# Four build steps' high one-hots in one VectorE operation, read by TensorE at every fourth element

## The chip, the core and the metric

The kernel runs on one core of a Trainium2 chip. The metric is the device time of one execution in microseconds; the lowest is the best. The core's engines are TensorE (PE, with PEld for loading its weights), VectorE (DVE), ScalarE (ACT), GpSimd (POOL) and SyncE (SP), each with its own instruction stream in order, which wait for one another by semaphores.

## The reference, cut to what matters

A graph of 6250 nodes has 200,000 edges, sorted by target. Three graph-convolution layers run over layer-normed node features of width 256, then a feed-forward layer over the half of the nodes that a router chooses.

```
def _gcn_conv(x, W, b, src, dst, norm, num_nodes):
    h = x @ W
    msg = h[src] * norm[:, None]
    agg = jax.ops.segment_sum(msg, dst, num_segments=num_nodes)
    return agg + b
...
h = jax.nn.relu(_gcn_conv(x, W1, b1, src, dst, norm, num_nodes))
h = jax.nn.relu(_gcn_conv(h, W2, b2, src, dst, norm, num_nodes))
return _gcn_conv(h, W3, b3, src, dst, norm, num_nodes)
...
x = x + _L0_gnn_ref(_layernorm(x, axis=-1), ...)
x = x + _L0_ffn_ref(_layernorm(x, axis=-1)[None], ...)[0]
```

## The kernel before

**The graph as a matrix.** The nodes lie in 49 tiles of 128. For the first 34 target tiles, which hold most edges, the kernel builds the adjacency matrix as counts (source in tile on the partitions, one row of 49 x 128 numbers a target tile) and multiplies it with the node features; the other tiles gather their edges' rows with indirect DMAs. The edges come in steps of 128. A target tile is cut into windows of 4 or 3 targets, and each window has a fixed quota of steps. In a build step (`step`, L1250) TensorE multiplies two one-hots of the step's 128 edges: the low one-hot `olo` (128 columns, source within its tile) as weights, the high one-hot `ohi` (49 source tiles x 4 or 3 targets, 196 or 147 columns) as moving operand, and adds into a PSUM window. ScalarE takes finished groups of windows out of PSUM (L1627, `evac_group`).

**Who writes the one-hots.** VectorE, in `one_hots(j)`, one call for each pair j of steps. Every even pair writes `olo` for four steps (L891): an is_equal of a table `iota_many`, in which each of 128 numbers stands four times, with four columns of `slo`, broadcast. Every pair writes `ohi` for its two steps (L894) in the same manner, from `iota_two`, in which each number stands twice. The results of a call are interleaved: the elements of one step stand four (`olo`) or two (`ohi`) apart. TensorE reads its operands at that distance. The ring holds RING = 8 pairs; the semaphore `used` counts steps that TensorE has done and `hot` the pairs that VectorE has written.

**The order of the work.** There are 1011 pairs. The first (the scan, j below SCAN) are built among the preparation of edges, degrees and first-layer products; VectorE's list there holds `unpack`, `digits`, `low_first` (L906) and others between the one-hots. From then on TensorE's list is written out by hand: after each pair come the units (dense matmuls of 512 columns, L1283, or gathered ones, L1295) that the table `DUE` names. VectorE's list follows the same table: after the one-hots of pair j come `sum_tile` (L923, L925), `low_tile` (L930) and `spot_steps` (L941) that are due by pair j - 5. The first sum of a layer frees the PSUM bank of the next unit.

**The overflow round.** At one place of each layer (`spill`) the kernel adds edges that did not fit a quota. GpSimd fetches an item and its rows (indirect DMAs L1849 to L1864; L1864 gathers rows of `row_dram`, which SyncE has stored before), compares (L1866 to L1870), and TensorE multiplies (L1326) at a fixed place of its list; all three engines of the round wait for one another. After it GpSimd goes on to `fetch_row` (L1890), the gathers of the sparse tiles.

**Other lines that are spoken of.** L1184 is the reciprocal of the roots of the degrees, for which ScalarE's L1731 must be done; L902 adds self-loops.

Of the kernel before, what the change touches and what calls it, by code (L numbers as in the profile page):

```python
# [8 lines left out]
ALU = mybir.AluOpType  # L9
# [3 lines left out]
F16 = mybir.dt.float16  # L13
# [3 lines left out]
P = 128  # L17
# [3 lines left out]
TILES = -(-N // P)  # L21
# [14 lines left out]
WC = W * TILES  # L36
# [14 lines left out]
WIDTH = [min(WIDTH_OF[t], P - i) for t in range(TD) for i in range(0, P, WIDTH_OF[t])]  # L51
# [17 lines left out]
WINDOW_OF = {FIRST[w] + i: w for w in range(WN) for i in range(QUOTA[w])}  # L69
# [49 lines left out]
RING = 8  # L119
# [4 lines left out]
HOTS = 24  # L124
# [302 lines left out]
def graph(nc, ctx, space, gathered_in, ones, route, small, smalli, b1_sb, br_b, x, x_turned, dst_rows, dst_over, dst_last, edges, gw, gb, wr, br, w1, b1, w2, b2, pair_dram, out):  # L427
    def sb(name, shape, dt=F32):
        return ctx.enter_context(nc.sbuf_tensor(name, shape, dt))
# [7 lines left out]
    area_a, area_b, area_r, area_t, area_g, area_w = (space[n][:] for n in ("a", "b", "ring", "tables", "rows", "work"))  # L437
# [9 lines left out]
    at = ET + 1 + ETILES  # L447
# [6 lines left out]
    at = (W + 1) * SBASE // 2  # L454
# [11 lines left out]
    at = 11 * D  # L466
# [23 lines left out]
    hots_area = sb("hots", [P, HOTS // 4, P, 4], F16)  # L490
    hots_f = hots_area[:].rearrange("p s n i -> p (s n i)").bitcast(F32)
    bias_rows = [hots_f[:, 0:D], area_w[:, 5 * D:6 * D]]
    key = area_t[:, 0:SBASE // 2].bitcast(F16)
    slo = area_t[:, SBASE:SBASE + SBASE // 2].bitcast(F16)
    at = SBASE + SBASE // 2
    ohi = area_t[:, at:at + RING * WC].bitcast(F16).rearrange("p (r n i) -> p r n i", r=RING, i=2)
    olo = area_t[:, at + RING * WC:at + RING * (WC + P)].bitcast(F16).rearrange("p (r n i) -> p r n i", r=RING // 2, i=4)
    at = TILES * P // 2
    xn = area_t[:, at:at + KC * D].rearrange("p (i d) -> p i d", i=KC)
# [26 lines left out]
    key_s, src_s = sb("key_s", [P, CHS * P], F16), sb("src_s", [P, CHS * P], I32)  # L526
    gw_sb, gb_sb = sb("gw_sb", [P, 3, HALVES, D]), sb("gb_sb", [P, 3, HALVES])
    ident, ident16, ones16 = sb("ident", [P, P]), sb("ident16", [P, P], F16), sb("ones16", [P, P], F16)
    zeros16 = sb("zeros16", [P, P], F16)
    iota16, iota_many = sb("iota16", [P, WC], F16), sb("iota_many", [P, P, 4], F16)  # L530
    iota_two = sb("iota_two", [P, WC, 2], F16)
    per_node = sb("per_node", [P, 8, TILES])
    dinv, factor, unfactor = per_node[:, 0], per_node[:, 1:4], per_node[:, 4:7]
    moments = sb("moments", [P, D])
# [28 lines left out]
    at = 0  # L563
# [4 lines left out]
    at = TILES * P  # L568
# [3 lines left out]
    at = len(BLOCKS[0]) * 2 * D  # L572
# [74 lines left out]
    pw = [ps(f"pw{i}", [P, 2, 512]) for i in range(2)]  # L647
# [42 lines left out]
    with nc.Block() as block:  # L690
        @block.vector
        def _(dve):
            def noted(ins, name=None):
                steps["all"] += 1
                if name:
                    steps[name] = steps["all"]
                ins.then_inc(c_dve, 1)

            def done(ins, name=None):
                noted(ins, name)  # L700
                dve.wait_ge(c_dve, steps["all"])
# [66 lines left out]
            lows(slice(0, 1))  # L768
            dve.wait_ge(c_pool, CONSTANTS + LATER_CONSTANTS)
            place_steps(0)  # L770
            done(dve.tensor_copy(iota_many[:], iota16[:, 0:P].unsqueeze(2).broadcast_to([P, P, 4])))
            noted(dve.tensor_copy(iota_two[:], iota16[:].unsqueeze(2).broadcast_to([P, WC, 2])))
            picks(False)

            def scales(l, bound):
# [106 lines left out]
                                            apply_absolute_value=True))  # L882

            def one_hots(j):
                r = j % RING
                if j >= RING:
                    dve.wait_ge(used, 2 * (j - RING + (2 if j % 2 == 0 else 1)))
                for t in LOOPS_OF.get(j, ()):
                    add_loops(t)
                if j % 2 == 0:  # L890
                    dve.tensor_tensor(olo[:, r // 2], iota_many[:], slo[:, 2 * j:2 * j + 4].unsqueeze(1).broadcast_to([P, P, 4]),  # L891
                                      ALU.is_equal)
                n = TILES * max(WIDTH[WINDOW_OF.get(2 * j + i, 0)] for i in range(2))
                dve.tensor_tensor(ohi[:, r, 0:n], iota_two[:, 0:n], key[:, 2 * j:2 * j + 2].unsqueeze(1).broadcast_to([P, n, 2]),  # L894
                                  ALU.is_equal).then_inc(hot, 1)

            def add_loops(n):
                dve.wait_ge(evac, PER_TILE * (n + 1))
# [34 lines left out]
            def spot_steps(n):  # L933
                if n == 0:
                    dve.wait_ge(stored_0, 16)
                    dve.wait_ge(stored_s, 32)
                    dve.wait_ge(pairs_clear, 16 * len(LATE_RUNS))
                if n >= HOTS // 4:
                    dve.wait_ge(g_used, SPOT_GROUPS[n - HOTS // 4][1])
                s = STEP_TILE[SPOT_GROUPS[n][0]]  # L940
                dve.tensor_tensor(hots_area[:, n % (HOTS // 4)], iota_many[:], key_s[:, s:s + 4].unsqueeze(1).broadcast_to([P, P, 4]),  # L941
                                  ALU.is_equal).then_inc(spot, 1)

            def measure():
# [275 lines left out]
        def _(pe):  # L1220
# [19 lines left out]
            def step(s):  # L1240
                w, j, i = WINDOW_OF[s], s // 2, s % 2
                v = GROUP_OF[w]
                t, a, b = EGROUPS[v]
                if s == FIRST[a] and v >= 2:
                    pe.wait_ge(evac, v - 1)
                if i == 0:
                    pe.wait_ge(hot, j + 1)
                half, at_c = (w - a) // PER_BANK[WIDTH_OF[t]], (w - a) % PER_BANK[WIDTH_OF[t]] * WIDTH_OF[t] * TILES
                n = WIDTH[w] * TILES
                pe.matmul(pw[v % 2][:, half, at_c:at_c + n], olo[:, j % RING // 2, :, j % 2 * 2 + i], ohi[:, j % RING, 0:n, i],  # L1250
                          start=s == FIRST[w], stop=s == FIRST[w] + QUOTA[w] - 1, skip_group_check=True).then_inc(used, 1)

            def pair(j):
# [854 lines left out]
```

## Time and profile before

| | |
|---|---|
| time of the runs, median of 3 (lowest, highest) | 1947.01 us (1945.54, 1950.79) |
| span of the profiled execution | 1945.7 us |
| PE busy | 1843.1 us (95%), 10171 matmuls |
| DVE busy | 1059.8 us (54%), 3304 instructions |
| ACT busy | 530.8 us (27%) |
| POOL busy | 1188.0 us (61%) |
| mean granted TensorE clock | 0.968 |
| build steps, L1250 | 2022 |
| high one-hots, L894 | 1011, 300.5 us busy, mean 330 ns |
| low one-hots, L891 | 506, 212.8 us busy, mean 420 ns |

The profiled execution's own time is its span and the little that lies around it: the median of the runs is 1.3 us above the span. Busy times are those of the whole span; which engine is late differs from stretch to stretch. A duration in the profile reaches from an instruction's start to its end, and the next one on the engine may start before that end, so what an instruction costs its engine in a full list is the distance between starts.

### The profile page before, as it was taken

To read this page: it belongs to the slowest core of one execution; us is meant where nothing else is said; L and a number is where in the kernel's file an instruction comes from. 1 tells how busy PE (TensorE), PEld (TensorE's weight loads), DVE (VectorE), ACT (ScalarE), POOL (GpSimd) and SP (SyncE) were. 2 spreads that over 40 slices of the span, in tenths; PEclk is the share of its full clock that TensorE was granted. 3 is DMA by queue.
4 is the path that set the end of the run, shared out by engine and by line. 5 is a ranking of instruction groups with operands and counts; after the bars stand their busy time and mean duration, and the time that the engine had idled before them with its cause. 6 is when DMAs were issued, how large, how long until landed. Compare 5 with 4: busy or idle time off the path is not lost.

```text
span 1945.7 us, 28922 instructions
## 1 busy us (share of the span) xinstructions
PE 1843.1 (95%) x10171; PEld 1070.5 (55%) x10171; DVE 1059.8 (54%) x3304; ACT 530.8 (27%) x1127; POOL 1188.0 (61%) x1178
## 2 busy tenths in 40 slices
PE   6875889999999999999999999999999999989998
PEld 5753556666555666645555555554444444446755
DVE  7777989888666666542222222213554456876422
ACT  5734234444444455512111111110000000002021
POOL 5401787688777676437777777745777777731301
PEclk9965889999999999999999999999999999999999
DMA  7568235555655566577677667756878888752200
GB/s 267 161 224 279 83 124 181 183 166 171 213 198 194 201 209 214 184 254 247 229 241 255 231 233 235 256 178 234 314 268 316 302 313 296 265 159 94 81 14 23
DMA packets 170453, 403.42 MB, mean 207 GB/s; under 512 B 29419, under 2 KB 122529, under 8 KB 157640
## 3 DMA queue, kind: packets, MB, share of 16 engines
q1 hardware_dynamic: 119720, 263.44, 37.9%
q0 software_dynamic: 50592, 138.13, 22.8%
q8 instruction: 85, 1.39, 0.3%
q14 instruction: 56, 0.46, 0.1%
HBM read 282.57 MB, written 118.89 MB: 206 GB/s over the span
## 4 chain that ended last, share of the span: by engine, by line
PE 84%; DVE 6%; issue 3%; POOL 3%; ACT 2%; DMA 1%; POOLq 0%; DVEq 0%; another core or an unknown queue 0%; ACTq 0%
PE ag L1283 29%; PE pw L1283 21%; PE ag L1295 10%; PE pw L1250 6%; PE pw L1379 3%; POOL space_rows L1864 2%; PE pw L1311 2%; PE both L1311 2%; PE ag L1392 2%; PE pw L1392 2%; PE ag L1379 2%; PE both L1303 1%; DVE space_tables L894 1%; PE ag L1236 1%; ACT space_ring L1627 1%
## 5 line engine op out<-in xcount | busy, mean ns | idle before, releaser
L1890 POOL DMA_INDIRECT space_rows<-row_dram,src_s x947 | 1006.4, 1063 | 335.3 <-issue 208.9
L1283 PE MATMUL ag<-space_a,space_ring 128*128 128x512 f16 x2107 | 623.2, 380 | 1.2 <-DVE space_work L925 1.1
L1250 PE MATMUL pw<-space_tables 128*128 128x147 f16 (+1 forms) x2022 | 330.0, 248 | 47.8 <-DVE space_tables L894 40.9
L1295 PE MATMUL ag<-space_rows,hots 128*128 128x512 f16 x947 | 358.5, 379 | 0.0
L1250 PEld LDWEIGHTS pw<-space_tables 128*128 128x128 f16 x2022 | 218.9, 116 | 233.1 <-DVE space_tables L894 65.1
L894 DVE TENSOR_TENSOR space_tables<-iota_two,space_tables 128x294 f16<-128x294 f16 (+1 forms) x1011 | 300.5, 330 | 0.0
L1627 ACT ACTIVATE space_ring<-pw 128x784 f16<-128x784 f32 (+1 forms) x257 | 220.4, 858 | 291.0 <-PE pw L1250 285.7
L1283 PEld LDWEIGHTS ag<-space_a,space_ring 128*128 128x128 f16 x2107 | 198.2, 97 | 99.8 <-DVE space_work L925 1.3
L891 DVE TENSOR_TENSOR space_tables<-iota_many,space_tables 128x512 f16<-128x512 f16 x506 | 212.8, 420 | 25.3 <-PE pw L1250 23.0
L1283 PE MATMUL pw<-space_b,space_ring 128*128 128x512 f16 x735 | 190.9, 379 | 0.0
L1283 PE MATMUL pw<-space_a,space_ring 128*128 128x512 f16 x686 | 168.7, 379 | 0.0
L1637 ACT ACTIVATE space_work<-space_work,per_node 128x256 f32<-128x256 f32 x147 | 73.8, 503 | 320.7 <-DMA space_work<-extra 320.6
L1295 PEld LDWEIGHTS ag<-space_rows,hots 128*128 128x128 f16 x947 | 107.3, 113 | 78.7
L930 DVE SCALAR_TENSOR_TENSOR space_a<-pw,per_node,space_a 128x256 f16<-128x256 f32 x49 | 23.7, 484 | 219.4 <-ACT space_a L1651 208.0
L1645 ACT ACTIVATE space_work<-both,gb_sb 128x128 f32<-128x128 f32 x196 | 61.3, 365 | 228.6 <-PE both L1303 228.4
L1283 PE MATMUL ag<-space_b,space_ring 128*128 128x512 f16 x441 | 115.9, 379 | 0.0
L1283 PEld LDWEIGHTS pw<-space_b,space_ring 128*128 128x128 f16 x735 | 71.8, 98 | 78.2
L1283 PEld LDWEIGHTS pw<-space_a,space_ring 128*128 128x128 f16 x686 | 67.3, 98 | 78.0
L941 DVE TENSOR_TENSOR hots<-iota_many,key_s 128x512 f16<-128x512 f16 x238 | 106.2, 459 | 1.3
L923 DVE SCALAR_TENSOR_TENSOR space_work<-ag,per_node,space_work 128x256 f32<-128x256 f32 x78 | 37.5, 481 | 101.6 <-PE ag L1283 57.5
L930 DVE SCALAR_TENSOR_TENSOR space_b<-both,per_node,space_b 128x256 f16<-128x256 f32 x49 | 23.7, 484 | 110.2 <-ACT space_b L1651 110.2
L1283 PE MATMUL pw<-space_a,space_tables 128*128 128x512 f16 x294 | 77.8, 388 | 0.0
(421 smaller groups left out, 1973.0 us busy)
## 6 DMA issues: line engine op xcount, KB each, us to landing
space_ring<-adj SPq DMA_DIRECT2D x48, 1568.0 KB, 7.5
adj<-space_ring SPq DMA_DIRECT2D x34, 1568.0 KB, 6.1
space_tables<-adj SPq DMA_DIRECT2D x17, 1568.0 KB, 7.8
extra<-hots SPq DMA_DIRECT2D x3, 6272.0 KB, 22.4
space_work<-extra SPq DMA_DIRECT2D x147, 128.0 KB
space_rows<-row_dram,src_s POOLq DMA_INDIRECT x947, 3.4
space_b<-in_x_turned SPq DMA_DIRECT2D x7, 896.0 KB, 13.6
space_a<-in_x SPq DMA_DIRECT2D x7, 896.0 KB, 6.1
```

What stands on the lines that cost most here:

```text
L891: dve.tensor_tensor(olo[:, r // 2], iota_many[:], slo[:, 2 * j:2 * j + 4].unsqueeze(1).broadcast_to([P, P, 4]), ALU.is_equal)
L894: dve.tensor_tensor(ohi[:, r, 0:n], iota_two[:, 0:n], key[:, 2 * j:2 * j + 2].unsqueeze(1).broadcast_to([P, n, 2]), ALU.is_equal).then_inc ...
L941: dve.tensor_tensor(hots_area[:, n % (HOTS // 4)], iota_many[:], key_s[:, s:s + 4].unsqueeze(1).broadcast_to([P, P, 4]), ALU.is_equal).the ...
L1250: pe.matmul(pw[v % 2][:, half, at_c:at_c + n], olo[:, j % RING // 2, :, j % 2 * 2 + i], ohi[:, j % RING, 0:n, i], start=s == FIRST[w], sto ...
L1283: mm = pe.matmul(bank(q), a[:, k, :], hh[l][:, k, :], start=i == 0 and not own, stop=i == TILES - 1)
L1295: pe.matmul(bank(q), hots_area[:, hot_at, :, g - SPOT_GROUPS[SPOT_GROUP_OF[g]][0]], slots[g % GR], start=False, stop=i == n).then_inc(g_us ...
L1311: mm = pe.matmul(ph[l - 1], fresh[:, q % 2, f, :], gw_sb[:, l, f, :], start=f == 0, stop=f == HALVES - 1)
L1379: mm = pe.matmul(bank_of(hidden_banks[h % 3])[:, 0:n], w1_sb[:, k, m * P:(m + 1) * P], xt[c][:, k, 0:n], start=k == 0, stop=k == HALVES - 1)
L1392: mm = pe.matmul(bank_of(out_banks[s % 2])[0:n, 0:D], hid[c % 2][:, m, i * P:i * P + n], w2_sb[:, m, :], start=m == 0, stop=m == HM - 1)
L1627: act.activation(target[:, :, d:d + n].rearrange("p s (h d) -> p s h d", h=2), pw[v % 2][:, :, 0:n // 2 * TILES].rearrange("p h (d s) -> p ...
L1637: act.activation(ep[:, q % 2], ep[:, q % 2], ACT.Copy, scale=unfactor[:, l, t:t + 1]).then_inc(e_scaled, 1)
L1890: pool.indirect_dma_start(slots[g % GR], None, row_dram[STEP_LAYER[g]], bass.IndirectOffsetOnAxis(src_s[:, s:s + 1], 0)).then_inc(g_in[g % ...
```

## The change

The high one-hots of four steps, two pairs, are written by one operation in place of two. The table `iota_two` goes; a table `iota_four` of 196 numbers, each four times, takes its place, and `iota_many` becomes its first 128 numbers. The ring keeps its size: 4 slots of four steps in place of 8 of two. Odd calls of `one_hots` write nothing and wait for nothing (they still add self-loops where those are due). The operation is as wide as the widest window of its four steps. `hot` counts groups of four steps, and TensorE waits for it once in four steps. TensorE reads the moving operand at every fourth element where it read every second. Weights, step order, windows and everything else stay.

```
-    ohi = area_t[:, at:at + RING * WC].bitcast(F16).rearrange("p (r n i) -> p r n i", r=RING, i=2)
+    ohi = area_t[:, at:at + RING * WC].bitcast(F16).rearrange("p (r n i) -> p r n i", r=RING // 2, i=4)
...
-    iota16, iota_many = sb("iota16", [P, WC], F16), sb("iota_many", [P, P, 4], F16)
-    iota_two = sb("iota_two", [P, WC, 2], F16)
+    iota16, iota_four = sb("iota16", [P, WC], F16), sb("iota_four", [P, WC, 4], F16)
+    iota_many = iota_four[:, 0:P]
...
-            done(dve.tensor_copy(iota_many[:], iota16[:, 0:P].unsqueeze(2).broadcast_to([P, P, 4])))
-            noted(dve.tensor_copy(iota_two[:], iota16[:].unsqueeze(2).broadcast_to([P, WC, 2])))
+            done(dve.tensor_copy(iota_four[:], iota16[:].unsqueeze(2).broadcast_to([P, WC, 4])))
...
             def one_hots(j):
-                r = j % RING
-                if j >= RING:
-                    dve.wait_ge(used, 2 * (j - RING + (2 if j % 2 == 0 else 1)))
+                r = j % RING // 2
+                if j % 2 == 0 and j >= RING:
+                    dve.wait_ge(used, 2 * (j - RING + 2))
                 for t in LOOPS_OF.get(j, ()):
                     add_loops(t)
                 if j % 2 == 0:
-                    dve.tensor_tensor(olo[:, r // 2], iota_many[:], slo[:, 2 * j:2 * j + 4].unsqueeze(1).broadcast_to([P, P, 4]),
+                    dve.tensor_tensor(olo[:, r], iota_many, slo[:, 2 * j:2 * j + 4].unsqueeze(1).broadcast_to([P, P, 4]),
                                       ALU.is_equal)
-                n = TILES * max(WIDTH[WINDOW_OF.get(2 * j + i, 0)] for i in range(2))
-                dve.tensor_tensor(ohi[:, r, 0:n], iota_two[:, 0:n], key[:, 2 * j:2 * j + 2].unsqueeze(1).broadcast_to([P, n, 2]),
-                                  ALU.is_equal).then_inc(hot, 1)
+                    n = TILES * max(WIDTH[WINDOW_OF.get(2 * j + i, 0)] for i in range(4))
+                    dve.tensor_tensor(ohi[:, r, 0:n], iota_four[:, 0:n], key[:, 2 * j:2 * j + 4].unsqueeze(1).broadcast_to([P, n, 4]),
+                                      ALU.is_equal).then_inc(hot, 1)
...
-                if i == 0:
-                    pe.wait_ge(hot, j + 1)
+                if s % 4 == 0:
+                    pe.wait_ge(hot, s // 4 + 1)
...
-                pe.matmul(pw[v % 2][:, half, at_c:at_c + n], olo[:, j % RING // 2, :, j % 2 * 2 + i], ohi[:, j % RING, 0:n, i],
+                pe.matmul(pw[v % 2][:, half, at_c:at_c + n], olo[:, j % RING // 2, :, j % 2 * 2 + i], ohi[:, j % RING // 2, 0:n, j % 2 * 2 + i],
```

## Rows read from the trace of the kernel before

**Rows 1.** Busy us (instructions) by stretch: PE, PEld, DVE, ACT, POOL; clock, DMA.

```profile
200.20:249.00 48.80, 46.69 (x327) 28.12 (x326) 48.80 (x181) 12.51 (x16) 43.98 (x1) 0.89 0.14 53
...
256.00:262.00 6.00, 6.00 (x25) 3.48 (x25) 2.72 (x6) 2.09 (x3) 2.56 (x3) 0.51 0.06 20
262.00:281.50 19.50, 17.74 (x145) 12.02 (x143) 19.31 (x75) 6.96 (x10) 17.27 (x3) 1.00 0.54 210
281.50:823.00 541.50, 537.26 (x3413) 340.69 (x3414) 397.71 (x1305) 261.34 (x423) 385.15 (x329) 1.00 0.57 191
```

**Rows 2.** Waits from 205 to 249 us: waited for, total us, times, longest.

```profile
PEld pw L1250 <- DVE space_tables L894: 10.5, 38, 0.4
```

**Rows 3.** Timeline of VectorE, 157 to 165 us: start, duration, idle time before.

```profile
164.22 0.47 DVE L1184 RECIPROCAL per_node<-per_node 128x49 f32<-128x49 f32 x1 [6.58 <-ACT per_node L1731]
```

**Rows 4.** Timeline of TensorE around the overflow round and at the first sum.

```profile
248.92 0.38 PE L1283 MATMUL ag<-space_a,space_ring 128*128 128x512 f16 x1
255.84 0.58 PE L1326 MATMUL both<-space_rows 128*128 128x512 f16 x1 [6.54 <-POOLq L1827]
...
281.54 0.39 PE L1283 MATMUL ag<-space_a,space_ring 128*128 128x512 f16 x1 [1.11 <-DVE space_work L925]
```

**Rows 5.** GpSimd: timeline of 205 to 300 us, and the page's group of L1890.

```profile
205.02 47.81 POOL L1864 DMA_INDIRECT space_rows<-row_dram,space_rows  x1 [36.41 <-DMA row_dram<-space_a]
...
264.77 16.70 POOL L1890 DMA_INDIRECT space_rows<-row_dram,src_s  x1 [0.99 <-POOL space_rows L1883]
...
L1890 POOL DMA_INDIRECT space_rows<-row_dram,src_s x947 | 1006.4, 1063 | 335.3 <-issue 208.9
```

**Rows 6.** Timeline of VectorE where the one-hots pause, 251 to 282 us.

```profile
251.43 0.59 DVE L894 TENSOR_TENSOR space_tables<-iota_two,space_tables 128x392 f16<-128x392 f16 x2
257.62 0.91 DVE L891 TENSOR_TENSOR space_tables<-iota_many,space_tables 128x512 f16<-128x512 f16 x1 [5.61 <-PE pw L1250]
...
281.00 0.48 DVE L925 SCALAR_TENSOR_TENSOR space_work<-ag,per_node,space_work 128x256 f32<-128x256 f32 x1
```

**Rows 7.** Timeline of VectorE in two stretches of nothing but one-hots.

```profile
216.74 0.42 DVE L891 TENSOR_TENSOR space_tables<-iota_many,space_tables 128x512 f16<-128x512 f16 x1
217.08 0.53 DVE L894 TENSOR_TENSOR space_tables<-iota_two,space_tables 128x294 f16<-128x294 f16 x2
217.52 0.42 DVE L891 TENSOR_TENSOR space_tables<-iota_many,space_tables 128x512 f16<-128x512 f16 x1
...
239.63 0.42 DVE L891 TENSOR_TENSOR space_tables<-iota_many,space_tables 128x512 f16<-128x512 f16 x1
239.97 0.64 DVE L894 TENSOR_TENSOR space_tables<-iota_two,space_tables 128x392 f16<-128x392 f16 x2
240.51 0.42 DVE L891 TENSOR_TENSOR space_tables<-iota_many,space_tables 128x512 f16<-128x512 f16 x1
```

**Rows 8.** Busy time by stretch of L891 alone, one per four steps.

```profile
166.30:200.20 33.90, 5.89 (x14) 0.50 1.00 330
200.20:249.00 48.80, 25.41 (x60) 0.89 0.14 53
```

**Rows 9.** Timeline of TensorE, 240.5 to 241.8 us.

```profile
240.59 0.38 PE L1283 MATMUL ag<-space_a,space_ring 128*128 128x512 f16 x1
240.81 0.34 PE L1250 MATMUL pw<-space_tables 128*128 128x196 f16 x2
240.99 0.38 PE L1283 MATMUL ag<-space_a,space_ring 128*128 128x512 f16 x1
```

**Rows 10.** Groups of weight loads, 281.5 to 823 us: busy us, mean ns, idle before.

```profile
L1250 PEld LDWEIGHTS pw<-space_tables 128*128 128x128 f16 x1414 | 159.5, 114 | 145.3 <-ACT space_ring L1627 9.3 <-DVE space_tables L894 0.8
L1283 PEld LDWEIGHTS ag<-space_a,space_ring 128*128 128x128 f16 x1381 | 126.7, 96 | 34.0 <-DVE space_work L925 1.3 <-issue 0.3
```

**Rows 11.** Groups of matmuls of the build in the same stretch.

```profile
L1250 PE MATMUL pw<-space_tables 128*128 128x196 f16 x864 | 146.8, 250 | 1.9 <-ACT space_ring L1627 1.9
L1250 PE MATMUL pw<-space_tables 128*128 128x147 f16 x537 | 81.3, 230 | 2.2 <-ACT space_ring L1627 2.1
```

More of the change, by code:

```diff
@@ L940, in spot_steps @@
                 s = STEP_TILE[SPOT_GROUPS[n][0]]
-                dve.tensor_tensor(hots_area[:, n % (HOTS // 4)], iota_many[:], key_s[:, s:s + 4].unsqueeze(1).broadcast_to([P, P, 4]),
+                dve.tensor_tensor(hots_area[:, n % (HOTS // 4)], iota_many, key_s[:, s:s + 4].unsqueeze(1).broadcast_to([P, P, 4]),
                                   ALU.is_equal).then_inc(spot, 1)
```

## The prediction

> **What bounds the kernel now.** I read the table of busy time by stretch first. The graph is built by 2022 "build steps" on TensorE, each multiplying a low one-hot (weights) with a high one-hot (moving operand); VectorE writes the one-hots, so the question in each stretch is which of the two is late. From 200.2 to 249 us VectorE is busy for 48.80 of 48.8 us while TensorE has idle left; from 281.5 us to the end of the build at 823 us TensorE is busy for 537.26 of 541.5 us and VectorE has 144 us free [rows 1]. So a cheaper VectorE can pay only before 281.5 us, and a dearer TensorE read is paid after it. The waits of 205 to 249 us say the same: TensorE's weight loads wait 38 times for the high one-hots of L894, 10.5 us in all [rows 2].
>
> Before 164 us the kernel is a chain of many engines. VectorE then stands idle for 6.58 us until ScalarE's root at L1731, which hangs on a round trip through GpSimd and DMA [rows 3]. Whatever VectorE gains earlier is spent in that wait, so I count nothing before 164 us.
>
> The odd place is 249 to 256 us. TensorE's last matmul starts at 248.92 us and the next only at 255.84 us, after 6.54 us of waiting for GpSimd's queue (the overflow round, "spill") [rows 4]. GpSimd's list shows why it is late: its gather at L1864 takes 47.81 us, while the same kind of instruction at L1890 takes 1.06 us on average over 947 of them [rows 5]. It starts at 205.02 us and ends at 252.83 us, 0.8 us after VectorE's uninterrupted one-hots end (251.43 + 0.59 = 252.02 us) [rows 5, 6]. The next long one ends at 264.77 + 16.70 = 281.47 us, just as VectorE's L925, which reads PSUM, ends at 281.48 us [rows 5, 6]. So in this trace a gather gets through when VectorE pauses from operations that read two SBUF tensors. The stall then sits where it does because TensorE stops, the ring of one-hots fills, VectorE halts and GpSimd is let in: it moves with TensorE's arrival.
>
> **The change, part by part.** *One high one-hot operation for two.* In the stretch with 147-column steps a group of four steps (one L891, two L894) takes VectorE 217.52 - 216.74 = 0.78 us; with 196 columns it takes 240.51 - 239.63 = 0.88 us [rows 7]. The two differ by 2 x 98 elements, so an element costs 0.10/196 = 0.00051 us. L891, whose operands have exactly the new operation's form (fourfold table, fourfold broadcast, 512 elements), takes 0.34 us start to start [rows 7], of which elements are 0.26; 0.07 to 0.08 us is fixed. The new operation keeps the elements and drops one fixed part: 0.07 us less for each group of four steps, 0.71 and 0.81 us in place of 0.78 and 0.88. That L891 runs at the same price per element excludes that the wider form falls to a slower rate.
>
> How many groups count: 14 between 166.3 and 200.2 us, 60 up to 249 us [rows 8], and 3 more while the ring's other slots fill. In the first stretch VectorE also has two other operations per pair and now and then waits for ScalarE, but those waits hang on VectorE's own earlier writes and move with it. 77 x 0.07 = 5.4 us earlier at 256 us. This holds only while TensorE can follow: two steps of 196 columns take 240.99 - 240.81 = 0.18 us and the dense matmul between pairs 240.81 - 240.59 = 0.22 us [rows 9], so four steps with two of those need 0.79 to 0.80 us against VectorE's new 0.81. It can, with almost nothing to spare.
>
> From 262 to 281.5 us VectorE is busy for 19.31 of 19.5 us [rows 1], and it ends with the tile's sum, for which TensorE waits 1.11 us [rows 4]. VectorE would be 23 x 0.07 = 1.6 us earlier, and TensorE gets the 1.1 us that it waited, no more. After that nothing: what VectorE saves from there on falls into its own free time.
>
> *The wait for the ring.* An odd pair waited for the same number of steps as the even pair before it (2(j - 6) in both), so dropping its wait frees nothing. Four slots of four steps hold what eight of two held. *Coarser hand-over.* The first pair of a group now gets its one-hot one half operation later (0.15 to 0.20 us, its extra elements), the second no later. Where TensorE waits for VectorE anyway the group's end decides, and it is earlier; where TensorE is the bound, VectorE is ahead in the ring and this costs nothing. *The table.* One copy of 784 elements replaces 512 and 392 before 164 us: nothing. Quads that straddle windows of unequal width write some columns more; there are few.
>
> *The moving read, every fourth element.* No row shows a moving operand read so. Below 0 there is no reason for it. The lower bound is 0: the present read of every second element makes 0.18 us for two steps of 196 columns, 0.09 each, and a contiguous 512-column matmul at 0.22 us scales to 0.084 [rows 9]; the doubling from one to two thus cost at most 0.006 us, part of it for loading weights. The upper bound is from weights that are already read at every fourth element: 114 ns a load against 96 contiguous, for 128 columns [rows 10], 0.14 ns a column, or 20 ns for 147 and 27 ns for 196 columns. For the 864 and 537 steps after 281.5 us [rows 11] that is 23.3 + 10.7 = 34 us. I take 0, because the moving read itself is the nearest row. One nanosecond a step would be 1.4 us; about 4.6 ns eat the whole gain.
>
> Row and rule differ here. The weights read at every fourth element are 18 ns dearer than contiguous ones [rows 10]. The Trainium skill ("Advanced Engine Details and Errata", SBUF Cachelines) asks for two hits on each 16-byte line for full speed and warns of a penalty where every access meets another line; f16 values at every fourth place leave exactly two. By the rule the sum below stays; by the row it ends 34 us higher. No run here shows the moving read itself.
>
> *Sum.* The profiled execution's span is 1945.7 us; the runs' median of 1947.0 lies 1.3 above. 5.4 + 1.1 = 6.5 us less gives 1939.2 for the span and **1940.5 us** for the median, 0.33% less. The measurement tells 0.3%, 5.8 us, from no change, so even the forecast lies near that edge.
>
> **Rivals.** *A: the strided read costs (the other side).* Place: TensorE's 1414 steps after 281.5 us, where nothing covers it. For: weights at that stride are dearer [rows 10]. Against: they are the only such sign. At 10 ns a step: 14.1 - 6.5, about 1955 us; at the upper bound 1974. It decides from 4.6 ns on, and is told from no change from 8.7 ns.
>
> *B: the overflow round does not move.* If L1864's 47.81 us is the gather's own time and not VectorE's doing, GpSimd still lets TensorE go at 255.8 us, less only the microsecond by which the gather may start earlier. Then the 5.4 us turn into a longer wait and 1.1 to 2.1 us remain: about 1945 us. For: GpSimd was waiting for a store's landing just before. Against: the two ends that meet VectorE's pauses [rows 5, 6].
> The Trainium skill ("SBUF — State Buffer", Who interferes with whom) speaks for B: it infers that a tensor_tensor takes only the shared read port and so does not hold up the writing of descriptors. In the trace the gather fares otherwise, 47.81 against 1.06 us, and the measurement decides for me.
>
> *C: GpSimd is let in early.* With 0.81 against 0.79 us a group VectorE is almost no longer the bound; if it fills the ring once between 205 and 249 us, the gather ends then and TensorE's gap of 6.7 us (255.84 - 248.92 less one matmul) goes too, and with it part of the 6 us at half clock that follow (granted 0.51) [rows 1, 4]. VectorE's own 5.61 us of idle time there [rows 6] is what can be used: 6 to 9 us more, 1932 to 1934 us. Against: at 0.02 us a group the ring does not fill in 60 groups.
>
> **How the numbers follow.** Forecast 0.57 (1938 to 1943), A 0.16, B 0.17, C 0.10. The bound for faster is 1941.2 us: the forecast gives 0.35 faster and 0.22 same, C 0.10 faster, B 0.17 same, A 0.13 slower and 0.03 same. So faster 0.45, same 0.42, slower 0.13. The range takes in C's lower end and B and cuts off most of A: 1931 to 1949.
>
> **What would show it.** Right: the high one-hots number 506 at about 0.46 and 0.56 us each (durations overlap the next start by about 0.08), groups at 0.71 and 0.81 us; TensorE's stall at the overflow round still some 7 us long but starting near 243.5 us; the sum's wait at 281.5 us gone; the build steps of 196 columns still 0.09 us apart. Wrong: build steps further apart between 300 and 823 us (A); the spill matmul still at 255 us after a longer wait (B); L1864 far shorter than 40 us and no gap (C).

## The result and the profile after

| | before | after |
|---|---|---|
| median of the runs (lowest, highest) | 1947.54 us (1945.54, 1950.79), 4 runs | 2064.02 us (2063.67, 2064.92), 4 runs |
| span of the profiled execution | 1945.7 us | 2062.4 us |
| build steps on TensorE: busy, mean | 330.0 us, 248 ns | 465.1 us, 324 ns |
| last build step starts at | 822.8 us | 938.9 us |

The changed kernel is slower by a factor of 1.0595 (95% interval 1.0578 to 1.0611): 116.5 us, where 6.5 us less were forecast. The last row of the table tells where to look: 116 of the 117 us of span are there when the build ends.

The busy time by stretch, as in [rows 1] (PE, PEld, DVE, ACT, POOL; clock, DMA):

```profile
200.20:249.00 48.80, 47.67 (x282) 32.43 (x283) 43.39 (x110) 10.87 (x14) 7.54 (x6) 0.92 0.15 58
...
281.50:823.00 541.50, 538.18 (x2858) 334.95 (x2857) 325.40 (x818) 209.47 (x343) 278.83 (x267) 1.00 0.46 155
```

From 281.5 us on TensorE is as full as before and at the same granted clock of 1.00, but in the same 541.5 us it gets through 2858 matmuls in place of 3413. So it waits no more than before; pieces of its work take longer. And before 249 us, where VectorE was the late engine, VectorE now has 5.4 us free and TensorE is the late one. The timeline of TensorE shows which piece; beside it [rows 9] has the same place before the change:

```profile
239.77 0.40 PE L1282 MATMUL ag<-space_a,space_ring 128*128 128x512 f16 x1
240.01 0.52 PE L1249 MATMUL pw<-space_tables 128*128 128x196 f16 x2
240.34 0.40 PE L1282 MATMUL ag<-space_a,space_ring 128*128 128x512 f16 x1
240.58 0.51 PE L1249 MATMUL pw<-space_tables 128*128 128x196 f16 x2
```

Two steps of 196 columns take 240.34 - 240.01 = 0.33 us (0.18 in [rows 9]), and the dense matmul behind them 0.24 (0.22). Worked out from the starts of all matmuls between 300 and 1000 us, a step of 196 columns costs 0.158 us before another step and 0.175 before a dense matmul (0.090 and 0.087 before the change), one of 147 columns 0.116 and 0.134 (0.069 and 0.067), and the dense matmul behind a pair 0.236 (0.215). Its own operands haven't changed, but the profile shows its weight loads longer too, 111 ns on average where [rows 10] has 96, while those of the build steps are as they were. Why the matmul behind a pair is longer was not tested. The weight loads (busy us, mean ns, idle before):

```profile
L1249 PEld LDWEIGHTS pw<-space_tables 128*128 128x128 f16 x1429 | 162.1, 114 | 151.8 <-ACT space_ring L1626 9.3
L1282 PEld LDWEIGHTS ag<-space_a,space_ring 128*128 128x128 f16 x1389 | 154.2, 111 | 70.1 <-DVE space_work L924 0.3
```

The sum comes near the loss. After 281.5 us there are 864 steps of 196 columns at 78 ns more (67 us), 551 of 147 at 57 ns (31 us), and behind some 707 pairs a dense matmul at 21 ns (15 us): 113 us. Step 600 starts 5.28 us later than before and the last one 116.15, so 110.9 us were lost in between.

GpSimd's gather of the overflow round is short now and TensorE no longer stops for it ([rows 4, 5]: 47.81 us, and 6.54 us of waiting):

```profile
204.63 5.36 POOL L1863 DMA_INDIRECT space_rows<-row_dram,space_rows  x1 [34.53 <-DMA row_dram<-space_a]
```

```profile
256.87 0.40 PE L1282 MATMUL ag<-space_a,space_ring 128*128 128x512 f16 x1
257.11 0.38 PE L1325 MATMUL both<-space_rows 128*128 128x512 f16 x1
```

### The profile page after: what moved, and what is told of

Its sections match the earlier page's. It is cut to its first block, busy times and chain, and to the rows that moved or that the text cites. A ratio compares the mean times of both kernels' runs of the same rounds, so it can differ in the third digit from the quotient of the medians.

```text
span 2062.4 us, 28274 instructions
## 1 busy us (share of the span) xinstructions
PE 1969.2 (95%) x10171; PEld 1146.2 (56%) x10171; DVE 1039.5 (50%) x2798; ACT 531.0 (26%) x1127; POOL 1094.1 (53%) x1178
## 4 chain that ended last, share of the span: by engine, by line
PE 89%; DVE 6%; ACT 2%; issue 1%; DMA 1%; POOL 0%; DVEq 0%
PE ag L1282 29%; PE pw L1282 20%; PE pw L1249 14%; PE ag L1294 10%; PE pw L1378 3%; PE pw L1310 2%; PE both L1310 2%; PE ag L1391 2%; PE pw L1391 2%; PE ag L1378 1%; PE both L1302 1%; ACT space_ring L1626 1%; PE ag L1235 1%; DMA space_rows<-in_dst_rows,tile_i 1%; PE both L1235 1%
## 5 line engine op out<-in xcount | busy, mean ns | idle before, releaser
L1889 POOL DMA_INDIRECT space_rows<-row_dram,src_s x947 | 949.8, 1003 | 497.6 <-PE ag L1294 303.5
L1282 PE MATMUL ag<-space_a,space_ring 128*128 128x512 f16 x2107 | 641.2, 385 | 0.0
L1249 PE MATMUL pw<-space_tables 128*128 128x147 f16 (+1 forms) x2022 | 465.1, 324 | 47.4 <-DVE space_tables L893 42.2
L1249 PEld LDWEIGHTS pw<-space_tables 128*128 128x128 f16 x2022 | 226.4, 115 | 231.9 <-DVE space_tables L893 50.7
L1282 PEld LDWEIGHTS ag<-space_a,space_ring 128*128 128x128 f16 x2107 | 227.2, 108 | 138.5 <-DVE space_work L924 0.3
L890 DVE TENSOR_TENSOR space_tables<-iota_four,space_tables 128x512 f16<-128x512 f16 x506 | 213.5, 422 | 95.0 <-PE pw L1249 91.3
L893 DVE TENSOR_TENSOR space_tables<-iota_four,space_tables 128x588 f16<-128x588 f16 (+1 forms) x506 | 256.7, 507 | 0.0
L1636 ACT ACTIVATE space_work<-space_work,per_node 128x256 f32<-128x256 f32 x147 | 73.5, 503 | 317.3 <-DMA space_work<-extra 317.3
L940 DVE TENSOR_TENSOR hots<-iota_four,key_s 128x512 f16<-128x512 f16 x238 | 106.4, 460 | 1.5 <-DVE aggr L975 0.2
```

Source lines behind the costliest of these rows:

```text
L890: dve.tensor_tensor(olo[:, r], iota_many, slo[:, 2 * j:2 * j + 4].unsqueeze(1).broadcast_to([P, P, 4]), ALU.is_equal)
L893: dve.tensor_tensor(ohi[:, r, 0:n], iota_four[:, 0:n], key[:, 2 * j:2 * j + 4].unsqueeze(1).broadcast_to([P, n, 4]), ALU.is_equal).then_in ...
L940: dve.tensor_tensor(hots_area[:, n % (HOTS // 4)], iota_many, key_s[:, s:s + 4].unsqueeze(1).broadcast_to([P, P, 4]), ALU.is_equal).then_i ...
L1282: mm = pe.matmul(bank(q), a[:, k, :], hh[l][:, k, :], start=i == 0 and not own, stop=i == TILES - 1)
L1636: act.activation(ep[:, q % 2], ep[:, q % 2], ACT.Copy, scale=unfactor[:, l, t:t + 1]).then_inc(e_scaled, 1)
L1889: pool.indirect_dma_start(slots[g % GR], None, row_dram[STEP_LAYER[g]], bass.IndirectOffsetOnAxis(src_s[:, s:s + 1], 0)).then_inc(g_in[g % ...
```

## The experiments

Two questions were put. Is it the read alone that costs, and by what rule? And what is VectorE's saving worth without it, which turned on GpSimd's overflow round? The times in the table are medians; the ratio is to the kernel before, run on the same chip.

| run | time | ratio (95% interval) |
|---|---|---|
| e_read_only | 2066.6 us | 1.0601 (1.0582 to 1.0620) |
| e_weights, e_sweep, e_lines | 2060.7, 2113.3, 2103.0 us | single runs, no ratio |
| e_split | 1936.7 us | 0.9937 (0.9922 to 0.9952) |
| e_split2 | 1936.8 us | 0.9947 (0.9929 to 0.9965) |
| e_pause, four pauses | 1952.2 us | 1.0017 (1.0007 to 1.0028) |
| e_pause2, two pauses | 1946.1 us | 0.9987 (0.9978 to 0.9996) |
| e_pause3, three pauses | 1940.9 us | 0.9959 (0.9945 to 0.9974) |
| e_best, e_split2 with two pauses | 1937.0 us | 0.9938 (0.9925 to 0.9952) |
| e_best3, e_split2 with three pauses | 1932.2 us | 0.9913 (0.9899 to 0.9927) |

**e_read_only: the new layout under the old operations.** The kernel before, with the distance alone changed:

```
-    ohi = ... .rearrange("p (r n i) -> p r n i", r=RING, i=2)
+    ohi = ... .rearrange("p (r n i) -> p r n i", r=RING // 2, i=4)
...
-                dve.tensor_tensor(ohi[:, r, 0:n], iota_two[:, 0:n], key...
+                dve.tensor_tensor(ohi[:, r // 2, 0:n, j % 2 * 2:j % 2 * 2 + 2], iota_two[:, 0:n], key...
...
-                pe.matmul(..., ohi[:, j % RING, 0:n, i],
+                pe.matmul(..., ohi[:, j % RING // 2, 0:n, j % 2 * 2 + i],
```

> The kernel before with its two VectorE operations for four steps, its waits and its hand-over per pair, but written into a slot interleaved by four, so that TensorE reads every fourth element. Theory 'the read': about 2065 us or a little more (up to 2072, since VectorE's saving is not there), steps of 196 columns 0.157 us apart. Rival 'the wide operation': about 1947 us as before.

Measured 2066.6 us, with 0.33 us for two steps:

```profile
240.05 0.52 PE L1250 MATMUL pw<-space_tables 128*128 128x196 f16 x2
240.38 0.40 PE L1283 MATMUL ag<-space_a,space_ring 128*128 128x512 f16 x1
```

The read alone makes the whole loss. The wider operation and the coarser hand-over, which this kernel doesn't have, would be worth the 2.6 us between it and the changed kernel, but the intervals of the two ratios overlap, so that is not shown.

**e_split: the wide operation under the old layout.** One operation for four steps writes two pairs side by side, each interleaved by two; the waits and the hand-over once in four steps are those of the changed kernel:

```
+                    four = key[:, 2 * j:2 * j + 4].rearrange("p (h i) -> p h i", h=2)
+                    dve.tensor_tensor(ohi[:, r:r + 2, 0:n], iota_two[:, 0:n].unsqueeze(1).broadcast_to([P, 2, n, 2]),
+                                      four.unsqueeze(2).broadcast_to([P, 2, n, 2]), ALU.is_equal).then_inc(hot, 1)
...
```

> One VectorE operation still writes the four high one-hots, but as two pairs side by side, each interleaved by two, so that TensorE reads every second element as in the kernel before. Theory 'the read' (TensorE's read at every fourth element is the whole loss, and the VectorE side of the prediction is right): build steps of 196 columns 0.09 us apart again, groups on VectorE at about 0.71 and 0.81 us before 249 us, about 1940.5 us, 6.5 us under the kernel before (down to 1934 if GpSimd's overflow gather gets in early, 1945 if it does not move). Rival 'the wide operation' (the coarser hand-over, or the one operation for four, is what costs): about 2064 us as after the change.

Measured 1936.7 us, between the forecast and rival C. VectorE's groups are what the sum said, 202.56 - 201.85 = 0.71 us here, and 0.81 with 196 columns:

```profile
201.85 0.41 DVE L891 TENSOR_TENSOR space_tables<-iota_many,space_tables 128x512 f16<-128x512 f16 x1
202.18 0.45 DVE L895 TENSOR_TENSOR space_tables<-iota_two,space_tables 128x588 f16<-128x588 f16 x1
202.56 0.41 DVE L891 TENSOR_TENSOR space_tables<-iota_many,space_tables 128x512 f16<-128x512 f16 x1
```

```profile
241.23 0.38 PE L1284 MATMUL ag<-space_a,space_ring 128*128 128x512 f16 x1
241.45 0.38 PE L1327 MATMUL both<-space_rows 128*128 128x512 f16 x1
241.66 0.34 PE L1251 MATMUL pw<-space_tables 128*128 128x196 f16 x2
241.84 0.38 PE L1284 MATMUL ag<-space_a,space_ring 128*128 128x512 f16 x1
```

Two steps are back at 0.18 us, and the overflow matmul (L1327) comes without a wait at 241.45 us, 14.4 us earlier than in [rows 4]. The gather got through early in this profile. It ends at 206.30 us, 0.82 us after the first break in VectorE's list since its start. That break is 0.04 us long (205.02 + 0.45 = 205.47, and the next start is 205.51):

```profile
203.09 3.21 POOL L1865 DMA_INDIRECT space_rows<-row_dram,space_rows  x1 [35.57 <-DMA row_dram<-space_a]
...
205.02 0.45 DVE L895 TENSOR_TENSOR space_tables<-iota_two,space_tables 128x588 f16<-128x588 f16 x1
205.51 0.42 DVE L891 TENSOR_TENSOR space_tables<-iota_many,space_tables 128x512 f16<-128x512 f16 x1
```

**e_weights: weights read contiguously, moving operand at every fourth.**

```
-  olo[:, j % RING // 2, :, j % 2 * 2 + i]
+  olo[:, j % RING // 2].rearrange("p n i -> p (n i)")[:, (j % 2 * 2 + i) * P:(j % 2 * 2 + i + 1) * P]
```

> The changed kernel, but TensorE loads the weights of a build step from 128 neighbouring elements in place of every fourth (so the counts that it builds are wrong, the work is the same). Theory 'the moving read alone': 2064 us within 5, steps of 196 columns still 0.157 us apart; loads at L1249 near 96 ns in place of 114. Rival 'weights and moving operand, both strided, get in each other's way': the step falls towards 0.09 us and the time towards 1945.

Measured 2060.7 us; a step of 196 columns takes 0.155 and 0.175 us, and the loads at L1249 are 97 ns (300 to 900 us):

```profile
L1249 PEld LDWEIGHTS pw<-space_tables 128*128 128x128 f16 x1288 | 124.7, 97 | 148.0 <-ACT space_ring L1626 7.0
```

The steps are 3 ns closer at most, so two strided operands in each other's way are not the cause.

**e_sweep: the moving operand at seven distances.** In the changed kernel each target tile reads at a distance of its own, each on its own line of the kernel:

```
+  hi = lambda k: slot[:, 0:TILES * k].rearrange("p (c k) -> p c k", k=k)[:, :, 0].unsqueeze(1).broadcast_to([P, g, TILES])
...
+EVERY = [1, 2, 3, 4, 6, 8, 16]
...
+  k = EVERY[t % len(EVERY)]
```

> The changed kernel, but TensorE reads its moving operand at a distance that goes with the target tile: every 1st, 2nd, 3rd, 4th, 6th, 8th or 16th element (49 of them, repeated 4 or 3 times; so the counts that it builds are wrong, the number of columns is the same). From the trace, distance from the second of two steps of 196 columns to the next matmul: 0.09 us at 1 and 2 and 0.157 at 4 by what the two kernels show. Theory 'two levels' (a read is at full or at half pace, half from a distance of 8 bytes on): 0.157 at 6, 8 and 16 as well, at 3 the one or the other or between. Rival 'the line' (the cost grows with the 16-byte lines that are touched): 0.12 at 3, 0.157 at 4, some 0.24 at 6 and 0.30 at 8 and 16. No time of the whole kernel is forecast.

The timeline of TensorE, two steps of 196 columns and the next dense matmul, at every 1st (L1256), 2nd, 4th, 6th, 8th and 16th (L1268) element:

```profile
886.67 0.34 PE L1256 MATMUL pw<-space_tables 128*128 128x196 f16 x2
886.84 0.38 PE L1301 MATMUL ag<-space_a,space_ring 128*128 128x512 f16 x1
...
403.41 0.35 PE L1258 MATMUL pw<-space_tables 128*128 128x196 f16 x2
403.60 0.38 PE L1301 MATMUL ag<-space_a,space_ring 128*128 128x512 f16 x1
...
447.71 0.52 PE L1262 MATMUL pw<-space_tables 128*128 128x196 f16 x2
448.05 0.40 PE L1301 MATMUL ag<-space_a,space_ring 128*128 128x512 f16 x1
...
476.31 0.69 PE L1264 MATMUL pw<-space_tables 128*128 128x196 f16 x2
476.81 0.40 PE L1301 MATMUL ag<-space_a,space_ring 128*128 128x512 f16 x1
...
508.35 0.86 PE L1266 MATMUL pw<-space_tables 128*128 128x196 f16 x2
509.04 0.40 PE L1301 MATMUL ag<-space_a,space_ring 128*128 128x512 f16 x1
...
547.05 0.87 PE L1268 MATMUL pw<-space_tables 128*128 128x196 f16 x2
547.74 0.40 PE L1301 MATMUL ag<-space_a,space_ring 128*128 128x512 f16 x1
```

Medians over all such rows, from the second step to the dense matmul, and the 16-byte lines that 196 columns touch:

| every | 1st | 2nd | 3rd | 4th | 6th | 8th | 16th |
|---|---|---|---|---|---|---|---|
| us | 0.086 | 0.092 | 0.137 | 0.180 | 0.264 | 0.350 | 0.353 |
| lines | 24.5 | 49 | 73.5 | 98 | 147 | 196 | 196 |
| ns a line | 3.5 | 1.88 | 1.86 | 1.84 | 1.80 | 1.79 | 1.80 |

"Two levels" falls; the line rules, at about 1.8 ns each (0.35 us at 8 and 16 where 0.30 was expected), and 0.44 ns a column is the floor beneath it. From the first step of a pair to the second the same reads take 0.162, 0.247 and 0.331 us at every 4th, 6th and 8th, so a line costs 1.65 to 1.8 ns by what follows the step. Every second element sits just above the floor (0.092 against 0.086 us); every fourth costs double. The dense matmul behind the pair takes 0.215 us at the 1st and 2nd, 0.222 at the 3rd and 0.236 to 0.237 from the 4th to the 16th: its surcharge does not grow with the lines.

**e_lines: the line or the jump, and the clock.** Other places of the moving elements in the changed kernel; the code shows the moving operand of each case. For some tiles of 196 columns: 4 neighbours in every 16 elements (49 lines); 2 neighbours in every 16, all of it twice (98 lines); the same 2 across a line's border (196 lines). For tile 0, whose 147 columns are built partly at half clock: every 8th element.

```
+  by16[:, :, 0:4]
+  twice(by16[:, :, 0:2])
+  twice(by16[:, :, 7:9])
+  by8[:, 0:TILES, 0].unsqueeze(1).broadcast_to([P, g, TILES])
```

> The changed kernel, with other places of the moving elements for some target tiles (the counts that it builds are wrong, the number of columns is the same). For 196 columns, distance from the second step to the next dense matmul. Theory 'the line' (a 16-byte line takes about 1.79 ns whatever the clock, a column 0.44 ns at the 2.4 GHz level; the larger counts): 2 neighbours in every 8 elements: 98 lines, 0.175 us. 4 neighbours in every 16: 49 lines, 0.09 us, though the span read is as long as at every fourth. 2 neighbours in every 16, all of it twice: 98 lines, 0.175 us; the same 2 neighbours across a line's border (elements 7 and 8): 196 lines, 0.35 us. Tile 0 (147 columns at every 8th element, granted clock 0.5): 0.26 us as in the sweep at the full clock. Rival 'the distance between neighbours' (each jump costs by its length): 4 neighbours in every 16 near 0.12 to 0.18 us, the border makes no difference, and tile 0 at half clock 0.5 us. No time of the whole kernel is forecast.

In this order, the first three:

```profile
452.31 0.34 PE L1261 MATMUL pw<-space_tables 128*128 128x196 f16 x2
452.48 0.38 PE L1300 MATMUL ag<-space_a,space_ring 128*128 128x512 f16 x1
...
473.90 0.52 PE L1263 MATMUL pw<-space_tables 128*128 128x196 f16 x2
474.23 0.40 PE L1300 MATMUL ag<-space_a,space_ring 128*128 128x512 f16 x1
...
407.31 0.86 PE L1265 MATMUL pw<-space_tables 128*128 128x196 f16 x2
407.98 0.40 PE L1300 MATMUL ag<-space_a,space_ring 128*128 128x512 f16 x1
```

Medians of the second step: 0.088, 0.178 and 0.347 us (and 0.175 for 2 neighbours in every 8), all as the line has it. Two neighbours cost double once a line's border lies between them, and four neighbours that lie far from the next four cost no more than the floor. Tile 0, with the granted clock of the stretch 193 to 197 us at 0.50:

```profile
194.23 2.28 PE L1257 MATMUL pw<-space_tables 128*128 128x147 f16 x8 [2.46 <-DVE space_tables L894]
197.24 1.22 PE L1257 MATMUL pw<-space_tables 128*128 128x147 f16 x4 [0.73 <-DVE space_tables L894]
```

```profile
193.00:197.00 4.00, 2.28 (x8) 0.91 (x8) 3.93 (x12) 3.63 (x10) 0.00 (x0) 0.50 1.06 368
```

Four more steps take 2.28 - 1.22 = 1.06 us, 0.265 a step, 1.80 ns a line: the same as in the sweep at the granted clock of 1.00 (0.263). The line's price doesn't go with TensorE's clock.

**e_split2: the weights at every second element too.** The low one-hots get the split layout of e_split.

> The split version, and the low one-hots laid out in the same manner, so that TensorE also loads its weights from every second element in place of every fourth. Theory 'the line' (TensorE fetches 16-byte lines at about 1.79 ns each, for weights as for the moving operand: 128 weights at every fourth element are 64 lines or 114 ns, at every second 32 lines or 57 ns, which is under the 96 ns of a contiguous load): loads at L1251 near 96 ns, two steps of 196 columns 2 to 3 ns closer, so some 3 to 4 us less than the split version, about 1933 us. Rival 'weights are always hidden behind the matmul before': as the split version, 1937 within 2.

The loads are 98 ns (114 in [rows 10]), as the line has it, and steps of 147 and 196 columns lie 2 and 1 ns closer:

```profile
L1252 PEld LDWEIGHTS pw<-space_tables 128*128 128x128 f16 x1368 | 132.5, 98 | 153.4 <-ACT space_ring L1629 9.5 <-DVE space_tables L896 0.4
```

The time, 1936.8 us, is that of e_split, as the rival had it: what the closer steps give (1 to 2 us) the runs don't show. In this profile the gather was held for 41.12 us, and the overflow round's stall was still there (6.08 us), but 8.8 us earlier than in [rows 4]:

```profile
202.92 41.12 POOL L1866 DMA_INDIRECT space_rows<-row_dram,space_rows  x1 [35.71 <-DMA row_dram<-space_a]
...
247.06 0.59 PE L1328 MATMUL both<-space_rows 128*128 128x512 f16 x1 [6.08 <-POOLq L1829]
```

So the stall moves with VectorE even where the gather is held, and the two profiles end alike (spans 1934.0 us in e_split, 1935.6 here): what e_split won at the overflow matmul it gave back in part at the tile's sum, where TensorE waits 3.61 us there and 0.6 here.

**e_pause: VectorE pauses while the gather runs.** The kernel before, and

```
+PAUSES = (150, 152, 154, 156)
...
+                if j in PAUSES:
+                    dve.wait_ge(used, 2 * j)
```

> The kernel before, with four short pauses of VectorE: at pairs 150, 152, 154 and 156 (about 206 to 211 us, just after GpSimd's gather L1864 has started) VectorE waits until TensorE has done all steps that are written. Theory 'VectorE holds the gather up' (and is let go by a pause): L1864 falls from 47.81 us to under 8 us, the overflow matmul no longer waits 6.5 us at 249 us, and with about 1 us for the pauses the time is some 1939 to 1942 us. Rival 'the gather takes that long by itself' (rival B of the prediction): L1864 still over 40 us, time 1947 to 1949 us.

```profile
204.23 3.29 POOL L1867 DMA_INDIRECT space_rows<-row_dram,space_rows  x1 [35.98 <-DMA row_dram<-space_a]
...
253.55 20.74 POOL L1880 TENSOR_TENSOR space_rows<-space_rows 128x256 f32<-128x256 f32 x1 [43.38 <-DMA space_rows<-extra,space_rows]
```

```profile
PE ag L1286 <- DVE space_work L928: 10.3, 1, 10.3
```

The gather falls from 47.81 to 3.29 us, and ends 0.8 us after the first pause begins, so VectorE held it up, and the wait at the overflow matmul is gone. But the time is 1952.2 us, over both forecasts. VectorE's one-hots no longer stop at 252 us, and so the next instruction of the round, GpSimd's addition of the sums, takes 20.74 us. The tile's sum needs its result, and TensorE's wait there (1.11 us in [rows 4]) grows to 10.3 us.

**e_pause2 and e_best: a second pause where the sums are added** (pairs 150 and 256).

> The kernel before with two pauses of VectorE in place of four: at pair 150 (about 206 us, which let GpSimd's gather through in 3.30 us in the run with four) and at pair 256 (just after the overflow matmul, when GpSimd adds the sums; in the run with four its addition then took 20.7 us under VectorE's one-hots, and TensorE waited 10.3 us for the tile's sum that hangs on it). Theory 'the stall only moves from one GpSimd instruction to the next that VectorE holds up': both go, the overflow matmul is 8 us earlier, the wait at the sum is back to 1 to 4 us, and the time is 1938 to 1942 us. Rival 'an early gather is worth nothing, the sum ends when VectorE's one-hots end': 1947 to 1952 us as with four pauses.

> The version with both one-hots split (one operation each for four steps, read at every second element) and the same two pauses of VectorE, at pairs 150 and 256. It had the overflow matmul wait for 6.08 us in its profile. Theory 'the stall moves': that wait and the one at the sum (3.61 us in the split version) go, less about 1 us for the pauses: some 1930 to 1934 us. Rival 'the two ends cancel': 1936 to 1938 us as without the pauses.

```profile
249.54 1.16 POOL L1880 TENSOR_TENSOR space_rows<-space_rows 128x256 f32<-128x256 f32 x1 [39.92 <-DMA space_rows<-extra,space_rows]
...
255.66 15.49 POOL L1885 TENSOR_SCALAR space_rows<-space_rows 128x1 f32<-128x1 f32 x1 [1.80 <-DMA extra<-space_rows]
```

The theory missed both times: 1946.1 us lies between theory and rival, and 1937.0 us where the rival had it. The addition takes 1.16 us now, but the round's last step, one number per partition, 15.49 (14.28 in e_best), and TensorE still waits 5.1 us (3.6) at the sum.

**e_pause3 and e_best3: a third pause, at pair 270.**

> The kernel before with a third pause of VectorE, at pair 270. With two, the next GpSimd instruction on the round's way (the step of its counter at L1885, after which the round is reported done) took 15.49 us under VectorE's one-hots, and TensorE waited 5.1 us at the sum. Theory 'the stall moves on to the next instruction that is held up': L1885 falls under 4 us, the wait at the sum falls by 3 to 5 us, and with 0.7 us for the pause the time is 1942 to 1944 us. Rival 'the sum only waits for VectorE's own one-hots before it': L1885 falls, but the wait at the sum and the time stay (1946 us).

> The same third pause in the version with both one-hots split and two pauses (1937.0 us, where the same GpSimd step took 14.28 us and TensorE waited 3.8 us at the sum). Theory 'the stall moves on': 1933 to 1935 us. Rival 'the sum only waits for VectorE's own one-hots': 1937 to 1938 us.

```profile
255.73 1.92 POOL L1885 TENSOR_SCALAR space_rows<-space_rows 128x1 f32<-128x1 f32 x1 [1.79 <-DMA extra<-space_rows]
```

```profile
PE ag L1286 <- DVE space_work L928: 1.2, 1, 1.2
```

1940.9 us, and 1932.2 us in e_best3, where the wait at the sum is 0.7 us: both a little better than expected. The stall had moved from one GpSimd instruction to the next, and TensorE hardly feels it when VectorE pauses at each of them. It has not gone: in e_pause3 the second gather behind the round takes 13.45 us, but TensorE does not wait for it before 300 us. e_best3 beats the kernel before by 16 us.

## Why the prediction was wrong

**The step that failed is "The moving read, every fourth element".** Its value of 0 and its upper bound of 34 us were both too small: it measured 78 and 57 ns a step, 98 us in all, and 113 us with the dense matmuls behind the pairs, for which the sum had no term. Rival A was right in kind, and priced at its upper bound at less than a third.

The lower bound went from one to two elements' distance and found almost nothing. The sweep shows why that says nothing of four: up to two the columns' own pace of 0.44 ns (196 x 0.44 = 86 ns) is the bound, and at two the lines (49 x 1.8 = 88 ns) have just come up to it. The floor hid a cost that had already grown to its height.

The upper bound took the difference between two weight loads, 114 - 96 ns in [rows 10]. A contiguous load is bound by something else at 96 ns (at every second element it is 98, in e_split2), so most of the 114 was hidden in the difference. Taken whole, 114 ns for 128 columns is 0.89 ns a column, two columns to a line of 1.8 ns; for 196 columns that is 175 ns, which is the pace measured. The right number stood in the row, read as a surcharge in place of a rate.

The rule drawn on beside it, of the Trainium skill ("Advanced Engine Details and Errata", SBUF Cachelines), has the mechanism right and the count wrong for this read: two columns from each 16-byte line ran at half pace at a granted clock of 1.00, the 2.4 GHz level, where four were enough (0.088 us in e_lines) and two and two thirds were not (0.137 us at every third). At a granted clock of 0.50, the 1.2 GHz level, two nearly do: between 166 and 200 us steps of 147 columns start 0.12 us apart before the change and 0.13 after it.

**What held.** *One high one-hot operation for two*: groups of 0.71 and 0.81 us, shown by e_split. Step 440 starts 6.4 us earlier there than before, but 3.3 of these are there by 162 us, where nothing was counted. e_split2 shows what the saving is worth at the overflow round: its overflow matmul, behind a stall that stayed and moved, starts 8.8 us earlier than before, 3.6 of these are there by 162 us, and 5.2 are left for the 5.4 forecast, its closer steps included. What VectorE's saving does before 162 us was not followed up. *The wait for the ring* and *Coarser hand-over* cost nothing that shows: without the read's price the same hand-over gives 1936.7 us.

**What held by half.** B fell: VectorE's one-hots hold the gather up, shown by a pause that frees it (47.81 to 3.29 us), and even where it stayed held, in e_split2, the round moved. The prediction's reading, that a gather gets through when VectorE pauses, holds for very short pauses too. In the eight runs in which the gather was held up to a break in VectorE's list, it ends 0.82 us after the first one, be it 5.6 us long (before, e_split2), a pause put in, 0.04 us (e_split) or 0.01 us (e_read_only). In the changed kernel, e_weights and e_sweep it ends without such a break (after 5.36, 5.35 and 29.98 us); what let it through there stays open.

The Trainium skill ("SBUF — State Buffer", Who interferes with whom) infers that a tensor_tensor does not hold up the writing of descriptors. The gather's 47.81 us go against that, unless it was the read of its row numbers from SBUF that was held, which no run here tells apart. For with both inputs in SBUF, the Trainium skill says in the same section, a tensor_tensor contends with GpSimd's reads; the addition (20.74 us) and the step on one number per partition (15.49 us) agree.

C's place was right and its price wrong: alone, an early gather makes the kernel before slower (1952.2 us; behind the four pauses TensorE is 2.9 us later than before), since the stall goes on to the next GpSimd instruction; only with all three held open does it give 7.5 us (1940.9 against 1948.4). That such holds, now long and now short, also make the spread of the unchanged kernel's runs (1944 to 1953 us) is likely and wasn't shown.

## What to carry to other kernels

Count the 16-byte lines that TensorE reads, and compare lines x 1.8 ns with columns x 0.44 ns (at a granted clock of 1.00): here interleaving the f16 moving operand by two cost next to nothing, by four it doubled a build step, and one VectorE operation could as well write two areas interleaved by two. To price an access pattern that the trace lacks, take the nearest row's whole rate, not its difference to a row that another limit holds up. Where an engine is starved by another, freeing one instruction moves the stall to the next one; follow the chain to its consumer before giving the gain a number.

## What the runs showed of the hardware

- A line of 16 bytes costs TensorE about 1.8 ns when the lines are the bound: for moving columns at a granted clock of 1.00 (every 8th element: 0.350 us for 196) and of 0.50 (0.265 us for 147), and for weights in the one case measured (114 ns for 64 lines).
- Behind a pair of such steps the next dense matmul takes 0.236 us in place of 0.215, and no more at every 16th element than at every 4th; dense weight loads take 111 ns on average in place of 96.
- VectorE's two-operand one-hots held up three kinds of GpSimd instruction: a gather (47.81 us), an addition (20.74 us) and a step on one number per partition (15.49 us). In eight runs the gather ended 0.82 us after the first break in VectorE's list, the shortest of them 0.01 us long (e_read_only).
- Not every GpSimd instruction is held: the compares behind the gather take 0.27 to 0.94 us in e_pause2, between one-hots without a break.
